# Four graph layers in one kernel: the scatter of sorted edges in three stages, and the last layer's lists loaded during the attention

## The reference, cut to what matters

```python
# L0: degree-normalised sum over the neighbours, then a linear map
agg = segment_sum(norm[:, None] * h[col], row);  x = x + agg @ W.T + b
# L1: attention over the edges, 4 heads of 32: softmax of leaky_relu(q[src] . k[dst]) by destination
x = x + segment_sum(alpha[..., None] * v[src], dst)
# L2: two weighted layers and a linear map
neigh = (segment_sum(h[src] * ew[:, None], dst) + h) / (count + 1)
h = leaky_relu(h @ Ws.T + bs + neigh @ Wn.T + bn + bias)          # twice;  x = x + h @ Wa.T + ba
# L3: every edge multiplies its source's row by a factor of its own 16 attributes
xw = h @ W;  ew = edge_attr @ edge_w                              # (103125, 16) @ (16, 128)
x = x + segment_sum(xw[src] * ew, dst) + b
```

## Time and profile before

| | |
|---|---|
| runs | 3122.51, 3131.64, 3140.24 us |
| profiled execution | 3137.08 us, of which the span is 3135.3 us |
| PE | 2324.6 us busy, 74% |
| DVE | 1929.2 us, 62% |
| POOL | 1985.7 us, 63% |
| ACT | 1301.7 us, 42% |
| granted TensorE clock | 0.875 of full over the span |

### The profile page before, as it was taken

One profiled execution on the slowest core, in us unless ns is written; L12 is line 12 of the kernel. 1 busy time (PEld: TensorE's weight loads), 2 busy tenths in 40 slices (PEclk: granted clock), 3 DMA queues, 4 the chain that ended last, 5 costly groups with the idle time before them and its releaser, 6 DMA issues. The chain is left out here.

```text
span 3135.3 us, 63975 instructions
## 1 busy us (share of the span) xinstructions
PE 2324.6 (74%) x22192; PEld 1705.1 (54%) x22192; DVE 1929.2 (62%) x3807; ACT 1301.7 (42%) x2282; POOL 1985.7 (63%) x1608
## 2 busy tenths in 40 slices
PE   3667677750039578787777788798993799999998
PEld 2466666640014245555555555553542587877776
DVE  7999999960023577777777777721112465656564
ACT  0466666650000377777777777500001222222221
POOL 2378878787772388788888888300000488887885
PEclk6799998875569679989999999999996799999998
DMA  6266666661146111111111111199692322222222
GB/s 77 95 168 188 185 185 180 186 186 15 11 99 160 59 48 46 42 45 42 45 45 45 45 44 41 39 228 221 140 213 9 66 55 61 55 56 55 54 56 56
DMA packets 219167, 285.61 MB, mean 91 GB/s; under 512 B 130289, under 2 KB 163960, under 8 KB 215725
## 3 DMA queue, kind: packets, MB, share of 16 engines
q1 hardware_dynamic: 170258, 246.53, 31.5%
q0 software_dynamic: 48720, 36.84, 6.2%
HBM read 171.50 MB, written 112.09 MB: 90 GB/s over the span
## 5 line engine op out<-in xcount | busy, mean ns | idle before, releaser
L385 POOL DMA_INDIRECT scratch_slots<-sort_pay,sort_slot x400 | 630.8, 1577 | 171.5 <-issue 171.2
L1796 POOL TENSOR_TENSOR score<-score,rise 125x500 f32<-125x500 f32 (+1 forms) x609 | 671.6, 1137 | 47.8 <-DVE peaks L1732 43.8
L2334 POOL DMA_INDIRECT gathered_rows<-scratch_projected,src_i x425 | 524.3, 1234 | 195.2 <-issue 194.6
L1732 DVE CUSTOM_DVE_ANT_0 score<-raw,log_in 125x500 f32<-125x500 f32 (+1 forms) x609 | 354.7, 619 | 151.9 <-PE raw L1617 87.8
L1679 ACT ACTIVATE rise<-raw 125x1000 f32<-125x1000 f32 (+1 forms) x350 | 314.3, 917 | 165.0 <-DVE peaks L1732 83.5
L1632 PE MATMUL probsT<-ident,score 125*125 125x125 f32 x2175 | 358.4, 294 | 29.8 <-ACT score L1688 13.1
L1632 PEld LDWEIGHTS probsT<-ident,score 125*125 125x125 f32 x2175 | 298.3, 200 | 106.8 <-DVE weighed L1753 67.0
L843 PE MATMUL built<-pair_weight,hot 125*128 125x125 bf16 x3750 | 265.5, 237 | 107.6 <-DVE pair_weight L790 107.6
L843 PEld LDWEIGHTS built<-pair_weight,hot 125*128 125x128 bf16 x3750 | 243.5, 107 | 123.7 <-DVE pair_weight L790 123.7
L790 DVE TENSOR_TENSOR pair_weight<-hot,w_parts 125x3840 bf16<-125x3840 bf16 x125 | 270.7, 2165 | 17.2
L1617 PE MATMUL raw<-QT,key 32*125 32x500 f32 (+1 forms) x1400 | 200.1, 642 | 93.3 <-DVE peaks L1732 90.2
(11 more groups left out here) (304 smaller groups left out, 4392.3 us busy)
## 6 DMA issues: line engine op xcount, KB each, us to landing
weights_in<-scratch_weightsT SPq DMA_DIRECT2D x50, 1093.8 KB
scratch_weightsT<-wT SPq DMA_DIRECT2D x25, 1367.2 KB
scratch_logs<-log SPq DMA_DIRECT2D x75, 437.5 KB
log_in<-scratch_logs SPq DMA_DIRECT2D x150, 218.8 KB
counts_in<-scratch_counts SPq DMA_DIRECT2D x25, 683.6 KB
scratch_counts<-cc SPq DMA_DIRECT2D x24, 683.6 KB
gathered_rows<-scratch_projected,src_i POOLq DMA_INDIRECT x425, 3.4
scratch_slots<-sort_pay,sort_slot POOLq DMA_INDIRECT x400
```

Source lines behind the costliest of these rows:

```text
L385: nc.gpsimd.indirect_dma_start(rows, bass.IndirectOffsetOnAxis(ap=sort["slot"][:, b, c:c + 1], axis=0), pay[:, c, :], None).then_inc(sort[ ...
L1732: nc.vector.tensor_tensor_reduce(out=score[u][h][:, at:at + w], in0=raw[:, h, 0:w], in1=log_in[:, at:at + w], scale=1.0, scalar=-3e38, op0 ...
L1796: nc.gpsimd.tensor_tensor(score[u][h][:, at:at + w], score[u][h][:, at:at + w], rise[:, b, h, 0:w], ALU.add).then_inc(added, 1)
L2334: nc.gpsimd.indirect_dma_start(gathered[:, g % GATHERS, k, :], None, projected, bass.IndirectOffsetOnAxis(ap=src_i[:, FIRST + g, k:k + 1], ...
```

## The change

- 9 blocks are sorted instead of 10. The last layer has 117 rounds and 93 items, and 465 gathers of 125 rows (58125 edges).
- The sorted blocks are placed in three stages: 0 to 4 in `adjacency`, 5 in the first layer, 6 to 8 in `weighted_layers`. Each stage's first attribute load is started in that stage. The buffers `sort_raw` and `sort_pay` are allocated by each stage; `sort_slot`, `sort_lo16` and `sort_rel16` stay for the whole program.
- `base_i`, `src_i`, `dst_i` (for the groups that aren't sorted), `mix` and `quad_mix` stand in buffers that are allocated before the attention. `mix` and `quad_mix` are set to zero in `one_over_degree`, and SP loads all five at the end of its part of `attention`. DVE works out relative destinations for those groups only. The lists of the 72 sorted groups, which only the general path reads, are loaded by SP at the end of the main block of `edge_layer`.
- The semaphores of the general path are cleared by POOL in `one_over_degree`.

```diff
-SORT_BLOCKS = 10
+SORT_BLOCKS = 9
-PLACED_IN_ADJACENCY = SORT_BLOCKS - 1
+GATHERED = SORTED // (EG * P)
+PLACED_IN_ADJACENCY = 5
+PLACED_IN_FIRST_LAYER = 1
+PLACED_EARLY = PLACED_IN_ADJACENCY + PLACED_IN_FIRST_LAYER
...
+def place_blocks(nc, T, pool, sort, slots, first, end):
+    nc.gpsimd.dma_start(sort["raw"][:], attribute_block(T, first)).then_inc(sort["raw_in"], 16)
+    for b in range(first, end):
+        place_block(nc, T, pool, sort, slots, b, end)
+    wait_placed(pool, sort, end)
...
# adjacency
-                place_block(nc, T, pool, sort, slots, b)
+                place_block(nc, T, pool, sort, slots, b, PLACED_IN_ADJACENCY)
...
# regular_gcn_layer
             clear_used(pool, used_before)
-            for b in range(PLACED_IN_ADJACENCY, SORT_BLOCKS):
-                place_block(nc, T, pool, sort, slots, b)
-            wait_placed(pool, sort, SORT_BLOCKS)
+            place_blocks(nc, T, pool, sort, slots, PLACED_IN_ADJACENCY, PLACED_EARLY)
...
# weighted_layers
+        @block.gpsimd
+        def _(pool):
+            place_blocks(nc, T, pool, sort, slots, PLACED_EARLY, SORT_BLOCKS)
...
+def fetch_last_layer(nc, T, sp, last):      # called at the end of SP's part of attention
+    with nc.allow_non_contiguous_dma(reason="runs of five edges, and one destination of every group"):
+        sp.dma_start(last["base_i"][:], T["dst"].rearrange("(o g r) -> o g r", o=1, r=EG * P)[:, :, 0]).then_inc(last["in"], 16)
+        for name, out in (("src", last["src_i"]), ("dst", last["dst_i"])):
+            sp.dma_start(out[:, GATHERED:, :], T[name][SORTED:].rearrange("(g p c) -> p g c", p=P, c=EG)).then_inc(last["in"], 16)
+    for k in range(EG):
+        sp.dma_start(last["mix"][k * EDIM:(k + 1) * EDIM, k, :], T["L3_gnn_edge_w"]).then_inc(last["in"], 16)
+    for k in range(4):
+        sp.dma_start(last["quad_mix"][k * SLOT:k * SLOT + EDIM, k, :], T["L3_gnn_edge_w"]).then_inc(last["in"], 16)
...
# one_over_degree
+        @block.gpsimd
+        def _(pool):
+            clear_used(pool, left)
+            nc.gpsimd.memset(last["mix"][:], 0.0)
+            nc.gpsimd.memset(last["quad_mix"][:], 0.0)
...
# edge_layer, preparing block: SP's loads of base_i, src_i, dst_i, mix and quad_mix and POOL's two memsets go
-                dve.wait_ge(edges_in, 48)
+                dve.wait_ge(last["in"], 16 * LAST_LOADS)
...
# edge_layer, main block, end of SP's part
+                    for name, out in (("src", src_i), ("dst", dst_i)):
+                        sp.dma_start(out[:, 0:GATHERED, :], T[name][0:SORTED].rearrange("(g p c) -> p g c", p=P, c=EG)
+                                     ).then_inc(last["in"], 16)
+                sp.wait_ge(last["in"], 16 * (LAST_LOADS + 2))
```

More of the change, by code:

```diff
@@ L2097, in general_edges, with edge_layer @@
                                   relative), of_pool_dmas=arrived)
-def edge_layer(nc, T, X, HT, W, ones, ident, iota, iota_tile, irregular, projected, block_base, slots):
+def edge_layer(nc, T, X, HT, W, ones, ident, iota, iota_tile, irregular, projected, block_base, slots, last):
     GATHERS = 5
@@ L2111, in edge_layer @@
     QROWS = QUAD * SLOT
-    assert FIRST * EDGES == SORTED and LISTS % 2 == 0
+    assert FIRST * EDGES == SORTED and FIRST == GATHERED and LISTS % 2 == 0
+    base_i, src_i, dst_i, mix, quad_mix = [last[k] for k in ("base_i", "src_i", "dst_i", "mix", "quad_mix")]
     with ExitStack() as c:
@@ L2181, in _ @@
             def _(sp):
[L2182 to L2190, removed]
                 sp.wait_ge(copied, len(quads()))
@@ L2327, in _ @@
                 assert b == SORT_BLOCKS
+                with nc.allow_non_contiguous_dma(reason="runs of five edges"):
+                    for name, out in (("src", src_i), ("dst", dst_i)):
+                        sp.dma_start(out[:, 0:GATHERED, :], T[name][0:SORTED].rearrange("(g p c) -> p g c", p=P, c=EG)
+                                     ).then_inc(last["in"], 16)
+                sp.wait_ge(last["in"], 16 * (LAST_LOADS + 2))
             @block.gpsimd
@@ L2615, in program @@
                 "p (b c) -> p b c", c=COLS)
[L2616 to L2623, removed]
-                                  sort, slots, used)
-                used = adjacency(nc, T, counts, logs, weightsT, ident, keys, w_parts, steps, out_degree, in_parts, sort, slots, used)
@@ new lines, in program @@
+            w_parts = hold(sb("w_parts", [P, WINDOWS // GRP, 3, 2 * GRP, 2], BF16))
+            steps = hold(sb("steps", [P, FULL], BF16))
+            used = window_starts(nc, T, table, starts, X, ident, ones, iota, iota_tile, irregular, sort)
+            used = edge_slots(nc, T, W, table, starts, X, H, norm, ident, keys, w_parts, steps, gathered, ones, irregular,
+                              sort, slots, used)
+            used = adjacency(nc, T, counts, logs, weightsT, ident, keys, w_parts, steps, out_degree, in_parts, sort, slots, used)
@@ L2631, in program @@
+        with nc.If(nc.values_load(irregular[0:1, 0:1], min_val=0, max_val=1) != 0):
+            left = general_adjacency(nc, T, all_counts, logs, weightsT, iota, iota_tile, out_degree, in_parts)
+            left += gcn_layer(nc, T, all_counts, X, H, W, ones, out_degree, sort, slots, used)
+        with nc.If(nc.values_load(irregular[0:1, 0:1], min_val=0, max_val=1) == 0):
+            regular_gcn_layer(nc, T, counts, X, H, W, ones, out_degree, sort, slots, used)
         per_node = keep(sb("per_node", [P, TILES]))
-        one_over_degree(nc, in_parts, per_node)
+        last = {"in": keep(nc.semaphore(unique("last_in"))), "base_i": keep(sb("base_i", [1, EGROUPS], I32)),
+                "src_i": keep(sb("src_i", [P, EGROUPS, EG], I32)), "dst_i": keep(sb("dst_i", [P, EGROUPS, EG], I32)),
+                "mix": keep(sb("mix", [EG * EDIM, EG, D])), "quad_mix": keep(sb("quad_mix", [4 * SLOT, 4, D]))}
@@ L2633, in program @@
+        one_over_degree(nc, in_parts, per_node, last, left)
         with ExitStack() as heads:
@@ L2639, in program @@
                 project(nc, HT, W, QT, keysT, V)
-            used = attention(nc, logs, keysT, X, H, QT, V, ident)
+            used = attention(nc, T, logs, keysT, X, H, QT, V, ident, last)
         with sb("HT", [D, LISTS * DEPTH]) as HT:
```

87 lines of the change are left out of this document (43 added, 44 removed).

## The result

In four runs each the changed kernel took 2948.78 us (2943.99 to 2955.38) and the kernel before 3135.94 (3122.51 to 3145.19), medians: a ratio of 0.941, 95% interval 0.937 to 0.945. The profiled execution took 2955.38 us, its span is 2953.6: 181.7 less than before. The forecast was 2958.

What follows compares the result with a forecast made beforehand. POOL's last four of nine adjacency blocks, nearly 200 us alone, bound the kernel most; then list waits and POOL's gathers. -193.8 - 46.4 - 3.5 + 8 + 59 + 1 = -175.7: 2961.4 us profiled, median 2958, range 2936 to 2984.

Steps and rivals of the forecast that it cites:

- Adjacency: In adjacency, five blocks instead of nine let SP end the stage at 708.1 instead of POOL at 901.9: -193.8 us.
- First layer: In the first layer, one block as before, POOL's last scatter at about 975 covered by PE until 1015: 0.
- Weighted layers: In the two weighted layers, three blocks' issue is hidden but their transfers beside the weight loads are not: +8 us.
- rival A: Weighted layers: scatters delay weight packets at full engine time, first pass +18 to +35, whole about 2980 us; chance 0.15.
- the mark I had set: Weighted layers: PE's waits for weights grow from 27.8 to about 35 us; reaching 50 would point to full engine time.
- the 17.6 us of the scatters' engine time: Weighted layers' first pass: upper end of the scatters' cost by DMA engine time, 0.11 x 160.
- after 2207 the share is 0.44: nothing more: Weighted layers: after 2207 us the DMA share is 0.44, so scatters there add nothing more.
- List loads: Head of the last layer: edge lists loaded earlier, so the rounding of row lists ends sooner: -46.4 us, bounds -44 to -48.
- rival C: Last layer: late lists' short runs beside the gathers make SP 7 us late, whole 2968 us; chance 0.07.
- Gathers: Last layer: 465 gathers for 425, with POOL setting the pace: +59 us, bounds +49 to +62.
- Rival B: Last layer: PE paces it, so the block shrinks by about 33 us instead of growing by 59, whole 2866; chance 0.04.
- Attention: In attention, list loads at its end fit where SP stands idle for 71.9 us before the barrier: 0.

Runs made afterwards that it cites:

- e5: Changed kernel with eight blocks placed in adjacency, one in the first layer, none in the weighted layers: 3055.1 us.
- e2: Changed kernel with ten sorted blocks, nine placed in adjacency and one in the first layer, leaving only the early list loads: 3108.9 us.
- e4: The kernel before, unchanged, profiled once more; its group's chip took 3155.4 us for it.
- e6: Changed kernel with eight blocks placed in adjacency, one in the first layer; weighted layers do three attribute loads but no scatters: 3062.1 us.
- e1: Changed kernel with the weighted layers' attribute loads and scatters held until 25 of the first pass's 35 weight slices are used: 2953.3 us, 0.938 of the kernel before.
- e7: Changed kernel with ten sorted blocks: six placed in adjacency, one in the first layer, three in the weighted layers: 2911.4 us, 0.931 of the kernel before.
- e3: Changed kernel with ten sorted blocks: 5 placed in adjacency, 1 in the first layer, 4 in the weighted layers: 2932.6 us, 0.930 of the kernel before.
- e12: Changed kernel with eleven sorted blocks (placed 6, 1, 4) and 28 idle DVE memsets in the first layer, timed again: 2888.5 us, 0.914 of the kernel before.
- e10: Changed kernel with eleven sorted blocks (placed 6, 1, 4) and 28 idle DVE memsets in the first layer, one run: 2836.9 us.
- e8: Changed kernel with eleven sorted blocks: 6 placed in adjacency, 1 in the first layer, 4 in the weighted layers: 2894.2 us, 0.927 of the kernel before.

## Why the prediction was right, step by step

*Adjacency* (-193.8, measured -199.4): right, and shown by e5: with three blocks more in the stage it takes 705.0, 128.9 longer. SP ended it, as the step said. The other 5.6 us are of the size by which the kernel before differs from one execution to another (769.8 in e2 and 771.9 in e4 for 775.5).

*First layer* (0, +2.6): POOL ended at 777.8, well before PE at 823.7, so the cover held; the fourteen profiles' first layers spread over 123.8 to 128.7 us, so this isn't told from nothing.

*Weighted layers* (+8, +16.9): the term that was mis-sized, and rival A is what the waits say by the mark I had set (51.8 us, past 50). Its price for the first pass (+18 to +35) was missed only just (+17.4), its mechanism is right only in part, and its whole time of 2980 us did not come. I had weighed the scatters' bytes against their engine time and left out what comes with them, three attribute loads of 0.32 MB each; e6 shows 8.5 us for those alone. So it is partly luck that the 17.6 us of the scatters' engine time lie so near to the 17.4. The step "after 2207 the share is 0.44: nothing more" was wrong too, as e1 shows. Taken over three executions the term is +11 to +19.

*List loads* (-46.4, -45.0): right; e2 shows it alone, but for the open 4 us in the attention. The late lists (rival C) ended 9.9 us ahead and not 15, and held nothing up.

*Gathers* (+59, +59.2 in the block): right for this pair, by 40 gathers at POOL's pace. It is not a constant: +56 between e7 and e5 on one chip, +37 between e3 and e1 on another, where PE's part ended the block with ten. Rival B, that PE paces, is false for nine blocks (POOL never waited for a message) and in part true for ten (e2 to e4) and eleven, where PE's part ends the block, though only in e12 did POOL wait long for messages (50.4 us).

*Attention* (0, -11.9): wrong by omission. I took a stage whose code and data the diff leaves alone as fixed. Two DVE instructions fewer in `edge_slots` move the loop's code, and each of ten turns stalls about 0.4 us less, 4 us in all; a turn comes every 73.6 us, for 74.5 in e3. What makes the other 8 us isn't told apart from the spread of one execution to the next, which was 12 us between e10 and e12. This error and that of the weighted layers cancelled each other, which is luck: the sum for the profiled execution (2961.4 us for 2955.4) is 6 us off, with one term 9 too low and one 12 too high.

Why a place stalls more than another was not settled in full. The Trainium skill (Runtime: NRT & Kernel Launch, section "Instruction fetch mechanics") says that instructions are streamed in sequential blocks, two of which are held, and that a taken branch whose target isn't held waits until it is fetched. The rows agree in that the stall stands at the turn alone, has no releaser, and vanishes at one place of the code together with the five packets of instructions a turn. That a body lying in fewer blocks is what helped in e10 is my inference; no run here shows which blocks are held, nor why e8's place costs 4.80 us and the changed kernel's 3.5 with five packets in both.

## What to carry to other kernels

Ask what ends each stage and move work to where its engine has room; that was worth 199 us here, where 194 were computed. When scattered work goes beside saturated loads, price everything that it brings, its own loads first. And look at the idle time put down to issue where a long loop turns: if it is there, a few idle instructions ahead of the loop, in a stretch where the engine waits anyway, are a cheap thing to try, and any edit ahead of the loop may change it unasked. The count of instruction packets on the profile's page told here whether it had worked.

## What the runs showed of the hardware

- A loop's turn on DVE cost 0, 3.5, 3.9 or 4.8 us by where its code lay, and the attention took 908 to 970 us for the same work (DVE 719 to 728 us busy). 28 memsets of one element removed the stall, and with it the five instruction packets of 8192 bytes a turn (56 on q14 in all for 106).
- Three contiguous loads of 0.32 MB beside weight loads at a DMA share near 1 cost 8.5 us (one execution of each), where bytes over the total rate give 4.5.
- Delaying the scatters and their loads into a pass with a DMA share of 0.44 at its start and 1.06 behind it only moved their cost: 6.7 us less there, 7.1 more here.
- Indirect gathers of 125 rows go at 1.53 to 1.54 us each on POOL in the seven profiles whose block they end, and at 1.56 to 1.66 in the seven where PE's part ends it; POOL's engine time for one was 1.20 to 1.21 (median) in each kernel.
- The last block of one program took 633 us at a clock of 0.99 and 673 at 0.97 over its gathers; POOL's waits for messages were 3.0 us in the one and 50.4 in the other. Whether the clock is the cause or goes with it isn't settled.
